# Writing the negated row maxima of attention scores straight into a 16-bit query word on Trainium2

## The reference, cut to what matters

```python
scores = jnp.einsum('bhqd,bhkd->bhqk', q, k) * SCALING + position_bias   # first attention
scores = jnp.where(causal, -jnp.inf, einsum(q, k) * scale)               # second attention
attn = jax.nn.softmax(scores, axis=-1)
ctx = jnp.einsum('bhqk,bhkd->bhqd', attn, v)
```

## Time and profile before

| | kernel before |
|---|---|
| median of three runs | 968.88 us |
| span of the profiled execution | 959.7 us |
| granted TensorE clock, mean | 0.966 of full speed |
| TensorE matmul busy | 834.5 us, 87% of the span |
| VectorE busy | 633.4 us, 66% |
| ScalarE busy | 553.3 us, 58% |
| GpSimd busy | 337.6 us, 35% |

### The profile page before, as it was taken

One profiled execution on the slowest core, in us unless ns is written; L12 is line 12 of the kernel. 1 busy time (PEld: TensorE's weight loads), 2 busy tenths in 40 slices (PEclk: granted clock), 3 DMA queues, 4 the chain that ended last, 5 costly groups with the idle time before them and its releaser, 6 DMA issues.

```text
span 959.7 us, 36375 instructions
## 1 busy us (share of the span) xinstructions
PE 834.5 (87%) x15215; PEld 507.8 (53%) x15215; DVE 633.4 (66%) x1534; ACT 553.3 (58%) x974; POOL 337.6 (35%) x451
## 2 busy tenths in 40 slices
PE   6879989989898988979888899987899789879995
PEld 3334444535444544545444455555555556768793
DVE  2547676975887687557757876567584656737773
ACT  3457657667765756745756566744548355425652
POOL 2442232222332342233324302436123544654452
PEclk9999999999999999979999899989999989989998
DMA  7997200000000000000000100011000111124634
GB/s 178 389 346 270 90 24 9 8 25 20 8 25 14 13 24 15 14 18 9 19 19 14 36 24 14 20 29 44 26 19 19 31 40 40 56 62 124 187 90 126
DMA packets 50191, 60.91 MB, mean 63 GB/s; under 512 B 5872, under 2 KB 36464, under 8 KB 49648
## 3 DMA queue, kind: packets, MB, share of 16 engines
q1 hardware_dynamic: 34768, 27.19, 9.7%
q10 hardware_dynamic: 10272, 21.14, 6.4%
q0 software_dynamic: 4992, 10.27, 3.2%
HBM read 22.92 MB, written 35.65 MB: 61 GB/s over the span
## 4 chain that ended last, share of the span: by engine, by line
PE 49%; DVE 27%; issue 9%; ACT 8%; another core or an unknown queue 3%; POOL 1%; DMA 1%; SPq 0%; POOLq 0%; DVEq 0%; ACTq 0%
DVE row_max L1337 13%; PE ps L928 9%; PE ps L755 5%; PE ps L788 5%; PE ps L1013 4%; PE ps L766 4%; PE ps L811 2%; PE ps L1005 2%; PE ps L802 2%; PE ps L1007 2%; PE ps L1006 2%; ACT probs L1165 2%; PE ps L773 2%; PE ps L794 1%
## 5 line engine op out<-in xcount | busy, mean ns | idle before, releaser
L1337 DVE TENSOR_REDUCE row_max<-ps 128x4 f32<-128x1024 f32 (+1 forms) x256 | 268.1, 1078 | 103.0 <-PE ps L766 42.1
L1165 ACT ACTIVATE probs<-ps 128x1024 f32<-128x1024 f32 x128 | 130.3, 1029 | 78.8 <-PE ps L788 56.3
L755 PE MATMUL ps<-bias_t,ch 64*32 64x512 f16 x2048 | 111.3, 395 | 24.8 <-DVE row_max L1337 10.9
L1653 POOL DMA_INDIRECT eo_rows<-eo_t,to_t x92 | 89.7, 975 | 114.5 <-ACT eo_t L1217 93.3
L1165 ACT ACTIVATE stage<-ps 128x1024 f32<-128x1024 f32 x96 | 96.8, 1026 | 29.7 <-PE ps L794 20.7
L1005 PE MATMUL ps<-xT_t,wgu_hi 128*128 128x256 f16 x276 | 78.0, 283 | 23.8 <-DVE row_max L1337 7.0
L1211 ACT ACTIVATE gate_t<-ps 128x256 f32<-128x256 f32 x138 | 52.6, 387 | 67.2 <-PE ps L1007 47.9
L1600 POOL TENSOR_TENSOR ctx_sb<-ctx_raw,ctx_sb 128x512 f32<-128x512 f32 x32 | 41.1, 1284 | 132.0 <-DVE ctx_sb L1365 131.8
L928 PE MATMUL ps<-probs,v_pad 128*32 128x256 f32 x1024 | 85.5, 400 | 1.8 <-ACT probs L1165 1.8
L1640 POOL DMA_INDIRECT slot_rows<-rows,slots x64 | 63.9, 998 | 57.1 <-DVE slots L1441 43.1
L1491 DVE SCALAR_TENSOR_TENSOR gate_s<-gate_t,ps 128x256 f32<-128x256 f32 x138 | 57.2, 415 | 33.9 <-ACT gate_t L1211 31.4
(11 more groups left out here) (170 smaller groups left out, 1603.3 us busy)
## 6 DMA issues: line engine op xcount, KB each, us to landing
slot_rows<-eo_g ACTq DMA_DIRECT2D x1, 12642.0 KB, 46.9
slot_rows<-eo_g ACTq DMA_DIRECT2D x1, 7998.0 KB, 25.9
x_t<-slot_rows SPq DMA_DIRECT2D x46, 129.0 KB
eo_g<-eo_rows SPq DMA_DIRECT2D x16, 256.0 KB
xT<-in_x SPq DMA_DIRECT2D x16, 128.0 KB, 2.1
kept<-resid SPq DMA_DIRECT2D x16, 128.0 KB, 1.7
resid_b<-kept SPq DMA_DIRECT2D x16, 128.0 KB
out_dram<-outT SPq DMA_DIRECT2D x16, 128.0 KB
```

The source lines that it names most:

```text
L755: eng.matmul(ps[HR * c:HR * (c + 1), two[r], :].rearrange("p (j s) -> p j s", j=2), csth("flip")[half, :], bias_t[half, way, 2 * g:2 * g + ...
L1165: eng.activation(probs[a][:, 2 * (k % 2):2 * (k % 2) + 2, :], both_of("c%d" % a, i, "e%d" % k), ACT.Exp).then_inc(z["exp"], 1)
L1337: ins = eng.tensor_reduce(row_max[a][:, qt, 4 * g:4 * g + 4].rearrange("p (r j) -> p r j", r=2), of_heads, AX.X, ALU.max)
L1653: eng.indirect_dma_start(out=eo_rows, out_offset=bass.IndirectOffsetOnAxis(ap=to_t[:, done % 4, t:t + 1].bitcast(U32), axis=0), in_=eo_t[: ...
```

## The change

VectorE's reduce writes minus the maximum itself, as a 16-bit word, into word 24 of `qk_tok` (stride 32 words, four heads per reduce). The table `row_max`, the step mx with both its instructions, its two semaphores and its wait are gone, and so is word 25 (its key row is zero now). TensorE's mxrows waits for the last reduce. GpSimd clears 32 words per partition instead of 64. In the planner the step mx is taken out and mxrows follows the reduces directly, so the whole plan is made anew.

```diff
@@ Plan.core @@
-        last = self.op((job, i, "mx"), "dve", 0.6, [(job, i, "m%d" % t) for t in range(len(SCORES[a]))])
-        last = self.op((job, i, "mxrows"), "pe", 0.48, [last], ONE)
+        last = self.op((job, i, "mxrows"), "pe", 0.48, [(job, i, "m%d" % t) for t in range(len(SCORES[a]))], ONE)
@@ block_kernel @@
-            row_max[a] = sb("row_max%d" % a, [P, KT, H])
@@ pe_core @@
-            eng.wait_ge(z["mxlo"], i + 1)
+            eng.wait_ge(z["max"], n_s[a] * (i + 1))
@@ dve_core @@
-                    ins = eng.tensor_reduce(row_max[a][:, qt, 4 * g:4 * g + 4].rearrange("p (r j) -> p r j", r=2), of_heads,
-                                            AX.X, ALU.max)
+                    word = qk_tok[a][:, b, qt, 0, 4 * g:4 * g + 4, 3 * HD].rearrange("p (r j) -> p r j", r=2)
+                    ins = eng.tensor_reduce(word, of_heads, AX.X, ALU.max, negate=True)
                 ins.then_inc(z["max"], 1)
-            yield at("mx")
-            slot = qk_tok[a][:, b, :, 0, :, :]
-            eng.wait_ge(z["max"], n_s[a] * (i + 1))
-            eng.tensor_scalar(slot[:, :, :, 24], row_max[a][:, :, :], -1.0, None, ALU.mult).then_inc(z["mxhi"], 1)
-            eng.wait_ge(z["mxhi"], i + 1)
-            eng.scalar_tensor_tensor(out=slot[:, :, :, 25], in0=row_max[a][:, :, :], scalar=-1.0,
-                                     in1=slot[:, :, :, 24], op0=ALU.mult, op1=ALU.subtract).then_inc(z["mxlo"], 1)
@@ pool_core @@
-            eng.memset(qk_tok[a][:, i % 2, :, 0, :, 3 * HD:3 * HD + 2], 0.0).then_inc(att[a]["clear"], 1)
+            eng.memset(qk_tok[a][:, i % 2, :, 0, :, 3 * HD], 0.0).then_inc(att[a]["clear"], 1)
@@ constants @@
-            ko[row + 24:row + 26, j] = 1
+            ko[row + 24, j] = 1
```

More of the change, by code:

```diff
@@ L491, in block_kernel @@
         q_rows, k_head, v_pad, probs = {}, {}, {}, {}
-        qk_tok, row_max, ctx_raw, ctx_sb, rden = {}, {}, {}, {}, {}
+        qk_tok, ctx_raw, ctx_sb, rden = {}, {}, {}, {}
         for a in (1, 2):
@@ L634, in block_kernel @@
         att = {a: signals("a%d_" % a, "qk v hi again vz lo kspread qspread krow qrow score max "
-                          "mxhi mxlo maxt clear qmax wscore exp pv ctx byq rec byd ctxn o") for a in (1, 2)}
+                          "maxt clear qmax wscore exp pv ctx byq rec byd ctxn o") for a in (1, 2)}
         x1_done, h2_done = sem("x1_done"), sem("h2_done")
```

## The result

The forecast was wrong, in size and in direction. On the first chip the changed kernel took 975.03 us (970.72 to 981.47, 20 runs) against 968.74 us (966.41 to 974.55, 20 runs): ratio 1.0066, interval 1.0050 to 1.0081. The time lies above the range (952 to 973). On three other chips, where the kernel before takes 891 to 894 us instead of 968, the same kernel was faster than before: 0.9952 (0.9933 to 0.9970), 0.9954 (0.9936 to 0.9971) and 0.9961 (0.9944 to 0.9977). There the direction of the forecast came true. Both results need explaining.

The account below looks back on a forecast made before the run. The kernel was taken as bound by TensorE, with holes from chains between TensorE, VectorE and ScalarE. Terms -6.1 (wait for mx) + 0 (reduce) + 0 (clear) gave 962.8 us against 968.9; 8-in-10 range 952 to 973.

Parts of the forecast that it names:

- that the order is kept: Assumption under the whole sum: the new plan keeps the traced order; other kinds of TensorE waits would prove it wrong.
- a deeper gain: New plan: all 21.8 us of planned latency between reduce and mxrows goes, giving 947.1 us; chance 0.08.
- a wait at the head of TensorE's queue: TensorE stands at mxrows for late reduces, 0.66 us each: 984 us, mild form 972.4; chance 0.17 over both.
- the 153 us behind the last core job: Stretch behind 807 us, without core jobs: claimed to hold nothing the change touches and to keep its length.
- -6.1 us for TensorE's wait at mxrows: TensorE's idle time before transposes L811 that ended with L1345, 6.1 us in 7 waits, taken as the gain.
- Third rival: mxrows at TensorE's queue head waits for late reduces: 984 us, or 972.4 in mild form; chance 0.17 over both.
- First rival: The new plan drops the whole planned latency between reduce and mxrows, 21.8 us, giving 947.1 us; chance 0.08.
- a period below 84 us: Repeating stretch, 85.4 us per two items: a fall below 84 would show the deeper gain by the new plan.
- Fourth rival: VectorE's reduce gets longer, by 0.047 us each (968 us) or 0.206 us (987 us); chance 0.05.
- The collision: Four L1345 beside GpSimd's L1600 hold VectorE some 1.06 us more each; none taken as inherited by another step.
- VectorE's busy time: Whole kernel: predicted to fall by 20.7 to about 612.7 us.
- The clear on GpSimd: 32 words instead of 64, 4.9 us in all before, nobody shown waiting: counted as nothing.

## Why the prediction was wrong, step by step

**The assumption of the sum: "that the order is kept".** This is the step that failed. The text said that the plan is made anew and gave the change of order two rivals, a deeper gain and a wait at the head of TensorE's queue; but the sum itself, and 0.56 of the chance, went by the traced order, which the changed kernel does not have. With it fell a premise of the text's first paragraph, that the 153 us behind the last core job "hold nothing that the change touches": from the last qmax to the end the kernel before takes 158.0 us, the changed code in the old plan 157.0 and the changed kernel 167.7. Kept in the old order, the change gained 5.2 us; the new order cost some 11.6 us on this kind of chip. The right reading would have been a direct gain of 6 us plus a change of order whose sign is open and whose size, by the spread of neighbouring plans, is some 8 us.

**-6.1 us for TensorE's wait at mxrows: right**, where the order is held (by the ratios 5.2 us, and 6.4, 7.7 and 6.7 us on the other chips). That it comes so near is in part luck: in two other orders the same code is worth some 9 and 16 us.

**Third rival, the wait at the head of the queue: it occurred, as one part.** The text set its mark at 6 us of waiting for the reduce at L811's line. It is 10.8 us in 12 waits, 0.90 each, above the 0.66 taken from the earlier trace rows, and 9.0 us in 10 waits on a chip with the short time. But there the whole kernel is still faster than before, so these waits alone don't turn the sign; with mx planned at 0.1 they are 1.3 us; and all waits for other engines at this line are 5.8 us less than before (13.5 against 19.3). They are a property of this one order, not of the missing step, and no run shows that they cost the kernel time.

**First rival, a shorter plan: wrong in what it took for granted.** It counted 32 x 0.68 us of planned latency as the most that the planner could gain. The planner lost 1.9 us by its own account. The text's sign for this rival, a period below 84 us, was even met in part (83.7 and 84.6 us), and the kernel was slower all the same. With a list scheduler there is no such bound, in either direction: a step less moves each later choice, and here 5.6 us more of expert work came to stand before the last hand-over.

**Fourth rival, a longer reduce: no.** 1.3 us, against 1.6 worked out from the earlier trace rows. The Trainium skill's rule on 16-byte lines (page "SBUF — State Buffer", section "Door 1: The DMA port swizzle") would make four outputs in four lines dearer; the measured 4 to 9 ns are all that can be due to it.

**The collision: not inherited.** The text took none of it back, and none came: the busiest candidate, the form of L1271 that reads two tables from SBUF (L1273 before), has 13.8 us in 32 instances against 16.1 us before, one of them of 1.503 us. Four of the 32 were 1.50 us long before. Counting every VectorE instruction more than 0.3 us above the median of its kind, the excess is 15.4 us before and 10.2 us now. And what no row could test now shows: 29 reduces ran beside the multiplication L1591 (L1600 before), and the longest took 1.231 us.

**VectorE's busy time: 616.7, not 612.7 us.** The text first counted that mx holds VectorE for 15.1 us because its instructions overlap their neighbours, and then took the full 20.7 us from the page's busy time. By the 15.1 it would have been 618.3.

**The clear on GpSimd** was to cost nothing more; it became longer (below), with nobody waiting.

## What to carry to other kernels

Where a scheduler makes the order, the trace of before tells what a change is worth only in that order: give the planner the old figures once, to time the code alone, and look at how far the planner's own end moves over small changes of one duration before you believe a gain of 1%. If that spread is larger than the gain, search for a good plan after each change, which here was worth about twice the change or more (1.9% against 0.7% on one chip, 0.9% against 0.5% on another). And time such a kernel on more than one chip: the sign of a 0.5% change differed between them.

## What was not expected of the hardware

- Chips of the same type differed by 8% in this kernel (968 against 891 us), with equal durations of VectorE and ScalarE instructions and mean granted clocks of some 0.957 and 0.983. The difference comes in steps: pauses within TensorE's runs of matmuls, mostly beside indirect transfers, and behind many of them 3.4 to 6.8 us at 1.2 GHz.
- Clearing 32 single 16-bit words per partition took GpSimd 0.240 us, clearing 64 in 32 pairs 0.153 us: half the words, 0.087 us more.
- A VectorE instruction of 0.302 us was stretched to 5.97 us by a GpSimd subtraction that began 0.17 us before it.
